# Decoder layer, one core: the cross attention's values are normalised on GpSimd instead of VectorE, under a new order of all engines

## What is computed

```
q = (queries @ Wq + bq).reshape(N, L, H, D)
k = (keys @ Wk + bk).reshape(N, S, H, D)
v = (values @ Wv + bv).reshape(N, S, H, D)
sm = jnp.einsum('nlhd,nshd->nlhs', q, k) / math.sqrt(D)
sm = jax.nn.softmax(sm, axis=1)
attn = jnp.einsum('nlhs,nshd->nlhd', sm, v).reshape(N, L, H * D)
return attn @ Wo + bo
```

## Time and profile before

| | us |
|---|---|
| median of 3 runs (1171.7 to 1174.6) | 1174.32 |
| the profiled execution, own time | 1172.56 |
| its span, first to last instruction | 1170.7 |
| PE busy in the span | 1021.1 (87%) |
| DVE busy | 986.5 (84%) |
| ACT busy | 889.3 (76%) |
| POOL busy | 465.3 (40%) |

### The profile page before, as it was taken

How to read it: one execution, slowest core, us unless ns; L and a number is a source line. 1 busy time by engine, 2 the same in 40 slices (tenths; PEclk the granted TensorE clock), 3 DMA queues, 4 the chain that set the end, 5 groups by cost and what they waited for, 6 DMA issues and landing times. The chain is left out here.

```text
span 1170.7 us, 28351 instructions
## 1 busy us (share of the span) xinstructions
PE 1021.1 (87%) x7826; PEld 839.7 (72%) x7826; DVE 986.5 (84%) x2175; ACT 889.3 (76%) x3030; POOL 465.3 (40%) x396
## 2 busy tenths in 40 slices
PE   1468999999999999999999999998759999897598
PEld 1346777777778777777778777776538988786598
DVE  6324998999999999999999999999754579989698
ACT  1356987998899889998899889987534579654695
POOL 0122543444434534444444443453310037587243
PEclk9879998999999999999999999999968999999799
DMA  6234766766676767776677667664500000000133
GB/s 169 60 93 139 200 166 159 191 179 181 164 189 177 185 165 183 183 184 177 171 186 178 183 163 190 172 183 115 143 12 1 1 1 0 1 1 1 48 106 98
DMA packets 138144, 149.15 MB, mean 127 GB/s; under 512 B 17282, under 2 KB 137826, under 8 KB 138088
## 3 DMA queue, kind: packets, MB, share of 16 engines
q1 hardware_dynamic: 136128, 148.04, 47.5%
q10 hardware_dynamic: 1960, 0.42, 0.4%
HBM read 94.47 MB, written 53.94 MB: 127 GB/s over the span
## 5 line engine op out<-in xcount | busy, mean ns | idle before, releaser
L577 POOL TENSOR_TENSOR Ph<-Px 125x448 f32<-125x448 f32 x128 | 147.1, 1149 | 295.5 <-ACT Px L669 295.5
L661 ACT ACTIVATE Px<-score,nmax_h 125x112 f32<-125x112 f32 x512 | 173.4, 377 | 35.1 <-DVE nmax_h L846 35.0
L650 ACT ACTIVATE Ps<-score,nmax_s 112x112 f32<-112x112 f32 x512 | 175.4, 415 | 0.1
L584 POOL TENSOR_TENSOR Ps<-Ps,rZs 112x896 f32<-112x896 f32 x64 | 107.8, 1703 | 92.7 <-DVE rZs L890 92.7
L846 DVE TENSOR_REDUCE nmax_c<-score 125x8 fp32r<-125x896 f32 x128 | 136.7, 1068 | 6.3 <-PE score L1137 6.2
L650 ACT ACTIVATION_READ_ACCUMULATOR Ps<-score,nmax_s 112x1 f32 x512 | 138.1, 270 | 0.0
L1137 PE MATMUL score<-QxS,KxS 96*125 96x224 f32 x768 | 134.2, 298 | 4.5 <-ACT Px L669 1.9
L669 ACT ACTIVATE Px<-score 125x896 f32<-125x896 f32 x128 | 119.9, 937 | 20.6 <-PE score L1148 13.6
L1160 PE MATMUL outX<-Px,Vn 125*32 125x224 f32 x1536 | 107.0, 367 | 15.0 <-DVE Vn L832 14.9
L1137 PEld LDWEIGHTS score<-QxS,KxS 96*125 96x125 f32 x768 | 104.1, 192 | 22.2 <-issue 13.5
L661 ACT ACTIVATION_READ_ACCUMULATOR Px<-score,nmax_h 125x1 f32 x512 | 118.4, 231 | 0.0
(11 more groups left out here) (225 smaller groups left out, 3103.1 us busy)
## 6 DMA issues: line engine op xcount, KB each, us to landing
KxS<-Kx_parts SPq DMA_DIRECT2D x192, 187.5 KB, 4.0
Kx_parts<-Kx SPq DMA_DIRECT2D x64, 375.0 KB, 3.8
ctx_in<-in_ctx SPq DMA_DIRECT2D x32, 375.0 KB
KsS<-Ks_parts SPq DMA_DIRECT2D x192, 56.0 KB, 2.1
QsS<-Qs_parts SPq DMA_DIRECT2D x96, 112.0 KB, 2.5
QxS<-Qx_parts SPq DMA_DIRECT2D x192, 56.0 KB, 3.2
Ks_parts<-Ks SPq DMA_DIRECT2D x32, 224.0 KB, 5.9
Qs_parts<-Qs SPq DMA_DIRECT2D x32, 224.0 KB, 2.2
```

Source lines behind the costliest of these rows:

```text
L577: pool.tensor_tensor(Ph[p][:], Px[u % NPX][:, :, 0:L // 2], Px[u % NPX][:, :, L // 2:L], ALU.add)\
L584: pool.tensor_tensor(Ps[:, h, :], Ps[:, h, :], rZs[:, h].rearrange("q (h o) -> q h o", o=1).broadcast_to([L, OCT, L]), ALU.mult)\
L650: ins = act.activation(Ps[:, g, :], score[slot][0:L, h // QUAD, (h % QUAD) * L:(h % QUAD + 1) * L], ACT.Exp, bias=nmax_s[:, g:g + 1], accu ...
L661: ins = act.activation(Px[u % NPX][:, h, :], score[SLOT_OF[f"C{u}"]][0:C, h // QUAD, (h % QUAD) * L:(h % QUAD + 1) * L], ACT.Exp, bias=max ...
```

## The change

`normalise_values` moves from DVE to POOL: it leaves the `step` of VectorE and enters that of GpSimd, six calls per batch. `reciprocal_cross` gets a wait for `vn_done` of the unit three earlier (its `rZc` buffer is now read on another engine), and `values_with_bias` one for `vn_done` of the batch two earlier (`Vx`). The pipeline gets a ninth stage, and the order of all five queues and of the PSUM banks is written anew. The core of the diff:

```diff
-STAGES = 8
+STAGES = 9
...
+            def normalise_values(n, u):
+
+                t, c = divmod(u, NC)
+                pool.wait_ge(rz_c, n.times(NU, u + 1))
+                wait_drain(pool, (n, f"V{c}"))
+                wait(pool, av_done, n.times(NU, u - (NPX - 1)))
+                pool.tensor_tensor(Vn[u % NPX][:], Vx[n.par][:, c, P * t:P * (t + 1)].rearrange("s (h e) -> s h e", h=OCT),
+                                  rZc[u % NPX][:].rearrange("s (h o) -> s h o", o=1).broadcast_to([C, OCT, HD]), ALU.mult)\
+                    .then_inc(vn_done, 1)
...
+                wait(dve, vn_done, n.times(NU, u - (NPX - 1)))
                 dve.reciprocal(rZc[u % NPX][:], Zc[u % NPX][:]).then_inc(rz_c, 1)
...
+                wait(dve, vn_done, n.back(2).times(NU, NC + c + 1))
                 dve.tensor_tensor(Vx[n.par][:, c, :], work[b][0:C, 0:D], brow["xbv"][0:C, :], ALU.add)\
...
 SP:
-                if n6:
-                    load_ctx(n6)
+                if n5:
+                    load_ctx(n5)
...
 PE:
-                if n4:
-                    transpose_ctx(n4, 0)
-                    transpose_ctx(n4, 1)
+                if n5:
+                    transpose_ctx(n5, 0)
+                if n6:
+                    transpose_probs(n6, 1)
+                if n5:
+                    transpose_ctx(n5, 1)
```

More of the change, by code:

```diff
@@ L782, in step @@
                 if n6:
-                    copy_probs(n6, 1)
-                if n4:
-                    hi_queries_cross(n4)
+                    copy_probs(n6, 0)
+                if n1:
+                    copy_x2T(n1)
                 if n6:
                     copy_probs(n6, 3)
-                if n0:
-                    copy_x2T(n0)
                 if n3:
                     exp_shifted(n3, 3)
+                if n5:
+                    hi_context(n5, 0)
+                if n6:
+                    copy_probs(n6, 1)
+                if n5:
+                    hi_context(n5, 1)
+                if n3:
+                    exp_by_head(n3, 4)
+                if n6:
+                    even_self(n6, 0)
+                if n5:
+                    hi_keys_cross(n5, 0)
+                if n6:
+                    even_self(n6, 1)
+                if n3:
+                    exp_shifted(n3, 5)
+                if n7:
+                    copy_values_self(n7)
+                if n8:
+                    copy_xT(n8)
+                if n7:
+                    exp_self(n7, 0)
+                if n8:
+                    hi_keys_self(n8)
+                if n4:
+                    exp_shifted(n4, 0)
+                if n5:
+                    copy_x1T(n5)
+                if n8:
+                    hi_queries_self(n8)
             iterations(act, step)
@@ L1007, in step @@
[L1007 to L1012, removed]
+                if n4:
+                    values_with_bias(n4, 2)
+                if n5:
+                    moments(n5, 0)
+                if n3:
+                    max_cross(n3, 2)
+                if n4:
+                    lo_with_bias(n4, "Qx", Qx, bcol["xbq"], qx_hi)
@@ new lines, in step @@
+                if n5:
+                    lo_context(n5, 0)
+                if n3:
+                    reciprocal_cross(n3, 2)
+                if n5:
+                    lo_context(n5, 1)
+                if n3:
+                    sum_cross(n3, 3)
+                    reciprocal_cross(n3, 3)
+                    max_cross(n3, 5)
+                if n6:
+                    pick_self(n6, 0)
+                if n5:
+                    add_eps(n5, 0)
+                    lo_keys_cross(n5, 0)
@@ L1040, in step @@
-                if n3:
-                    max_cross(n3, 4)
+                    reciprocal_cross(n3, 4)
+                if n5:
+                    norm_self(n5)
+                if n2:
+                    mean_variance(n2, 1)
+                if n6:
+                    residual(n6, 0)
+                if n5:
+                    values_with_bias(n5, 1)
+                if n2:
+                    add_eps(n2, 1)
+                if n3:
+                    sum_cross(n3, 5)
+                if n8:
+                    lo_with_bias(n8, "Ks", Ks, bcol["abk"], ks_hi)
@@ new lines, in step @@
+                if n6:
+                    transpose_probs(n6, 1)
+                if n5:
+                    transpose_ctx(n5, 1)
+                if n3:
+                    cross_scores(n3, 5)
+                    cross_values(n3, 1)
+                if n6:
+                    self_values(n6, 0)
+                    self_values(n6, 1)
+                if n5:
+                    keys_cross(n5, 0)
+                if n3:
+                    cross_values(n3, 2)
+                    cross_values(n3, 3)
+                    shift(n3, 5)
@@ new lines, in step @@
+                if n7:
+                    self_scores(n7, 0)
+                    project_values_self(n7)
+                if n8:
+                    transpose_x(n8)
+                if n4:
+                    cross_scores(n4, 0)
+                if n6:
+                    project_out_self(n6)
+                if n5:
+                    values_cross(n5, 1)
+                if n8:
+                    project_T(n8, "Ks", w["aWk"], xT, "xT")
+                if n4:
+                    shift(n4, 0)
@@ L1281, in _ @@
+                if n5:
+                    transpose_x1(n5)
+                if n7:
+                    self_scores(n7, 1)
+                if n8:
+                    project_T(n8, "Qs", w["aWq"], xT, "xT")
+                if n4:
+                    cross_scores(n4, 1)
             iterations(pe, step)
```

280 lines of the change are left out of this document (89 added, 191 removed), and 6 rows, old and new, of the table WORK_USES.

## The result

The changed kernel takes 1196.25 us (median of 4 runs, 1190.40 to 1199.16), the kernel before 1174.45 in the same comparison: ratio 1.0192, 95% interval 1.0166 to 1.0219. It is 21.8 us slower; the forecast was 1181 us, 6.7 above the 1174.32 shown ahead of it. The profiled execution took 1198.82 us (span 1197.0), 26.3 us more than that of before (span 1170.7).

The account below looks back on a forecast made before the run. DVE, 95.4% busy, was taken as the bound before; after, a loop through the context load of 11.1 + 2.9 + 2.8 + 7.3 = 24.1 us against 23.82, times 31 steps, adds 8.7 to 1172.6: 1181 us, range 1140 to 1218.

Parts of the forecast that it names:

- the ring: Each context load depends on the previous one through ACT, DVE, SP and DRAM, once per step: 24.1 us, bounding the period.
- the save of Ks to KsS: SP's transfer of Ks from save to landing, ahead of the KsS lays: 2.9 us, bounds 1.9 and 6.0.
- the landing of the context: Context load from issue to landing, with other transfers issued behind it: 7.3 us, bounds 5.2 and 9.3.
- the term of 11.1 us: From landing of the context load through PE's transposes, ACT's work and Ks on DVE: 10.5 us plus 0.6 of waiting.
- the filling: Partly filled steps at each end of the pipeline with the ninth stage: counted 0, bounds -10 and +10 us.
- what leaves DVE: Six Vn at 582 ns cost DVE 3.5 us of a step; without them it needs 19.2 us.
- PE as the next bound at 22.85 us: With DVE relieved, PE's busy time per step, 22.85 us at most, would bound the kernel next.
- the best rival: Faster: context load lands in 6 us, save of Ks in 2, period PE's 22.8 us, 1141 us; chance 0.30.
- the move by itself: Vn from DVE to POOL, if this were all: a step some 1.0 us shorter, 31 us in 31 steps.
- The signs named ahead: Profile after: DVE about 80%, POOL's Vn about 0.5 us, context transposes waiting 1 to 3 us, SP's longest wait for Ks_parts.

Follow-up runs that it names:

- The 8 fillers: Changed kernel plus 8 small identity transposes on PE ahead of its wait for the context load, result untouched: 1185.72 us.
- the new order with the ring open: Changed kernel with the context load issued first in SP's step, behind the save of Ks: 1143.65 us; the same with Vn back on DVE: 1152.34 us.
- the kernel with waits of 3.4 us in each step: Changed kernel with the context load moved one place back in SP's queue, behind the three lays of QsS: 1286.02 us.

## Why the prediction was right or wrong

**Right: the ring and its place; its length in part by luck.** The direction came out, but the loss is some three times the forecast: 26.3 us in place of 8.7. The chain through context, Ks and KsS bounds the step; 24.1 us were forecast and 24.39 measured, and opening it at one place gives 52.6 us back. Two terms were too long (the save of Ks to KsS 2.3 in place of 2.9, the landing of the context 6.9 in place of 7.3) and one too short, 12.27 in place of 11.1. That the sum came within 0.3 us is luck in so far as a missing 1.2 us was made up by 1.0 us too much in those two.

**Wrong: the term of 11.1 us.** Summed from rows of before it holds to within 0.6 us where the clock is full (11.65). It left out that PE can lose its clock behind a wait: in 7 of 16 steps the same chain takes 13.07. I took the durations of the chain from a trace with a granted clock of 1.00 and used them in a kernel in which I myself had PE wait about 2 us in each step. The 8 fillers put this at some 0.7 us of a step between 300 and 700 us.

**Wrong: the filling, "I count 0".** This is the step that failed most. I multiplied the difference of 24.1 and the steady 23.82 by 31, though the earlier trace rows had already told me that filling steps are shorter. They take 166.1 / 8 = 20.8 us in the mean before, some 24 us less in all eight than steady steps, where I had read 12 off the context loads; and a ring is as long in the filling as anywhere: there it costs the difference to a short step. Opening the ring takes back 11.9 of the 14.3 us lost there. What is left of the filling without the ring lies within my bounds of 10 us: with Vn on DVE at the same 0.29 to 0.30 us, the new order with the ring open enters the ninth batch 169.1 us after the first (40.9 to 210.0), the old order 161.9 (40.9 to 202.8), so 7 us. These two kernels differ in the whole order and not only in the ninth stage; no run tells the two apart. The lines of the transposes of x, up to the ninth batch, of these two kernels:

```profile
L1084 PE MATMUL work<-ident,x_in x18: 257/261/449, 40.9 to 210.0; 112*128 112x112 f32 x18
```

```profile
L1075 PE MATMUL work<-ident,x_in x18: 257/288/446, 40.9 to 202.8; 112*128 112x112 f32 x18
```

**The sum again.** 31 x 0.28 = 8.7 was forecast. It is 23 x 0.54 = 12.5, 14.3 for the filling and -0.5 for the rest: 26.3 between the two profiled executions, 21.8 between the medians.

**Half right: what leaves DVE.** The 3.5 us of a step do leave it, and the earlier trace rows did show that a Vn waits behind POOL. But I booked all of it to the engine, when about half belonged to the place in the queue (582 against 291 to 303 ns); the new order removes that half even with Vn on DVE.

**Wrong, without effect on the forecast: PE as the next bound at 22.85 us.** I called it "at most" and then used it as the floor of the range and of the best rival. A step of 21.87 us was run, in which PE is busy 99.9%; the move by itself, put at 31 us, is worth 4.8% or some 56. The rival's 1141 us stands close to the 1143.65 of the opened ring, but not by its reason: the steps were shorter (22.21) and the filling longer.

**The signs named ahead.** DVE at 80% and POOL's Vn at 0.40 to 0.42 us (estimate 0.45, taken 0.5) came true, and so did the context's transposes waiting in every step, though for 0.3 to 1.9 us and not 1 to 3. SP's longest wait did not: I had put the load of x and the wait for Qs behind the landing of Ks_parts, not beside it. The Trainium skill's factor of about two for GpSimd (GPSIMD Engine Reference, "3.1 Elementwise — side-by-side cycle accounting"), measured there at 2048 elements, would make, by estimate, 0.58 us of DVE's undisturbed 291 ns; the trace says 0.40, a factor of 1.4, and the measurement decides.

**Left open.** Why the new order with the ring open stays behind the old order with the same move (1143.65 against 1118.21). Of the 23.1 us between the two profiled spans (1140.3 and 1117.2) 9.8 lie in the filling (168.5 against 158.7 us to the ninth batch), 11.0 from there to the last batch and 2.3 behind it. Which part of the order costs them was not tried.

## What to carry to other kernels

When a change moves a load from stages ahead into the step of its use, follow what must land before it can be issued, and close the loop: a ring costs in every step, in the short filling steps most. Before an operation is moved off a full engine, see what it waits for there: here putting it elsewhere in its own queue gave 2.8%, moving it alone 4.8%, and moving it with a new order of everything lost 1.9%. Change the engine and the order in separate steps.

## What was not expected of the hardware

A wait of PE of 1.93 us was followed by 3.4 us at the lower level of its clock, in a stretch (300 to 700 us) that runs at full clock but for seven such drops; the work behind it took 1.4 us longer (13.07 against 11.65), and in the kernel with waits of 3.4 us in each step nearly every step had such a drop. Work of no use in the gap gave 10.5 us back with 8 transposes, which mostly ended before the data came, and 3 us with 16, which mostly did not. And a Vn on VectorE that starts while Ps or Ph is running on GpSimd ends only 0.15 us behind it (51 of 51), while one that starts during `rstd` is not held up (17 of 17).
